# Second graph layer: gathered rows are weighted and split into high and low parts on VectorE and ScalarE, and one 512-column rounded matmul takes the place of the 256-column full-precision matmul with a weighted one-hot

## The chip, the cores and the metric

The kernel runs on one core of a Trainium2 chip. The metric is the device time of one execution in microseconds. Three runs of the kernel before gave 1801.48 (median), 1800.02 and 1804.83 us.

## The reference, cut to what matters

A graph of 3125 nodes with 256 features and 50,000 edges, sorted by destination, goes through two layers. The first is a typed attention layer with a residual and a layer norm. The second, which the change touches, is

```python
all_msg = jnp.einsum('nf,rfo->rno', h, weight)          # 16 relations
msg = all_msg[rel_type, src] * norm                     # norm: one weight per edge
gate = jax.nn.sigmoid(all_gate[rel_type, src])[:, None]
msg = msg * gate
agg = jax.ops.segment_sum(msg, dst, num_segments=n_nodes)
x = _layernorm(x + jax.nn.relu(agg))
```

## The kernel before, in words

Nodes are cut into 26 rounds of 121. An edge window of 2048 edges belongs to each round, 128 partitions by U = 16 "chunks" of one edge per partition. The kernel first builds tables, then runs the attention layer round by round, and on the way writes `message_table`: for each node and relation, the gated message of 256 f32 values. All of that stays as it was.

The second layer starts when the last messages are in the table. It is a loop of its own over the 26 rounds, written out in blocks of four turns (`Turn`, `turns`). The order on each engine is the order in which its block of code issues, and engines meet at semaphores alone. In each round:

- GpSimd (POOL, `gather_messages`, line 651) issues 16 indirect DMAs. Each takes its 128 row numbers from `rows` in on-chip memory and brings 128 rows of 1 KB from `message_table` into a chunk of `mrows`. `mrows` has LB = 4 buffers of a round each; before it fills one again, POOL waits until TensorE has done the round that used it (`l_agg`, `r.again`).
- VectorE (DVE, `weigh_onehot`, line 1524) builds, two rounds ahead, 16 weighted one-hot matrices of 128x121 with one TENSOR_SCALAR each: 1 where the edge's destination is this node, times the edge weight. It has four buffers too.
- TensorE (PE, `l1`, line 954) waits for each half of the round's rows, then sums the edges into nodes with 16 matmuls of f32 operands, 256 columns each. The trace shows two matmul records for each of these.
- `finish` (lines 1504 to 1515, DVE, with a square root on ScalarE, ACT, at line 1176) does relu, residual and layer norm of the round, and SyncE (SP) loads the residual and stores the result (`l1` and `last` in the SP block).

In the attention layer the same kinds of work stand beside each other: POOL gathers at line 637, DVE's `make_onehot` (line 1359) makes 16 one-hots in one operation from two broadcast operands, and `weigh` (line 1458) multiplies 128x1024 values four times in a row. `low_part` (line 1239) is the subtraction that makes the low part of a split, after ACT has copied the high part into a rounded type (`F32R`). The profile gives `mrows` the name of `kv`, the memory that it lies in.

## Time and profile before

| what | value |
|---|---|
| median of three runs | 1801.48 us |
| profiled execution, span | 1798.2 us |
| its own time beside the span | not given; the median run is 3.3 us longer than the span |
| second layer, first gather to end of span | 1179.3 to 1798.2 us |
| PE / DVE / ACT / POOL busy, whole span | 74% / 51% / 27% / 50% |
| gathers of the second layer | 416, of 0.951 us each, 1.25 us from start to start |
| matmul records of the second layer | 832, of 0.463 us each |

Busy shares are averages over stages with different limits; the second layer is read from stretches of its own. Waits named "remote" are for semaphores set by another engine whose work the profile doesn't pair with the wait. Some matmul records are missing from the trace, so that a PE which runs on without a break can look idle; PE's "issue" time in the second layer is mostly that.

### The profile page before, as it was taken

To read this page: it belongs to the slowest core of one execution; us is meant where nothing else is said; L and a number is where in the kernel's file an instruction comes from. 1 tells how busy PE (TensorE), PEld (TensorE's weight loads), DVE (VectorE), ACT (ScalarE), POOL (GpSimd) and SP (SyncE) were. 2 spreads that over 40 slices of the span, in tenths; PEclk is the share of its full clock that TensorE was granted. 3 is DMA by queue.
4 is the path that set the end of the run, shared out by engine and by line. 5 is a ranking of instruction groups with operands and counts; after the bars stand their busy time and mean duration, and the time that the engine had idled before them with its cause. 6 is when DMAs were issued, how large, how long until landed. Compare 5 with 4: busy or idle time off the path is not lost.

```text
span 1798.2 us, 21483 instructions
## 1 busy us (share of the span) xinstructions
PE 1322.6 (74%) x6758; PEld 1088.5 (61%) x6758; DVE 921.7 (51%) x1914; ACT 492.7 (27%) x1069; POOL 890.4 (50%) x905
## 2 busy tenths in 40 slices
PE   5799999458999999999999999943424444444444
PEld 4788888447878787878787888732313323332333
DVE  5744444468777777787878787221212222222222
ACT  3222222304454545454444444500000000000000
POOL 1041000476565656565656563057576666666661
PEclk9899999769999999999999999965556666666666
DMA  7454446566676767776767675333333333333331
GB/s 143 130 152 145 135 133 225 151 191 181 209 238 210 238 208 232 217 238 207 238 211 238 209 239 161 106 111 110 87 110 99 105 102 103 104 103 103 104 102 44
DMA packets 103851, 286.56 MB, mean 159 GB/s; under 512 B 20805, under 2 KB 40409, under 8 KB 100661
## 3 DMA queue, kind: packets, MB, share of 16 engines
q0 software_dynamic: 56032, 169.34, 31.5%
q1 hardware_dynamic: 47774, 116.71, 21.3%
q8 instruction: 19, 0.31, 0.1%
q14 instruction: 26, 0.20, 0.0%
HBM read 189.33 MB, written 96.65 MB: 159 GB/s over the span
## 4 chain that ended last, share of the span: by engine, by line
PE 56%; issue 24%; DVE 7%; DMA 6%; POOL 3%; ACT 1%; SPq 1%; another core or an unknown queue 1%; DVEq 0%; ACTq 0%; POOLq 0%
PE bank L954 14%; PE bank L837 11%; PE bank L865 10%; PE bank L795 5%; PE bank L729 5%; DMA kv_table<-tstage 4%; PE bank L783 2%; POOL kv L651 2%; PE bank L813 2%; PE bank L751 2%; PE bank L737 1%; DVE kv L1367 1%; PE bank L757 1%; POOL kv L637 1%; DVE S L1372 1%
## 5 line engine op out<-in xcount | busy, mean ns | idle before, releaser
L637 POOL DMA_INDIRECT kv<-kv_table,rows x416 | 458.6, 1102 | 304.9 <-PE bank L865 130.9
L651 POOL DMA_INDIRECT kv<-message_table,rows x416 | 395.7, 951 | 264.7 <-issue 123.5
L954 PE MATMUL bank<-kv,onehot_w 128*121 128x256 f32 x832 | 276.1, 463 | 336.7 <-issue 300.8
L954 PEld LDWEIGHTS bank<-kv,onehot_w 128*121 128x121 f32 x832 | 186.6, 226 | 426.2 <-issue 389.8
L837 PE MATMUL bank<-wr_r,x1T_r 128*121 128x512 f32 x1248 | 324.8, 403 | 2.2 <-ACT mstage L1098 2.2
L837 PEld LDWEIGHTS bank<-wr_r,x1T_r 128*121 128x121 f32 x1248 | 217.7, 183 | 51.9 <-ACT mstage L1098 3.3
L1504 DVE SCALAR_TENSOR_TENSOR z<-bank,xb 121x256 f32<-121x256 f32 x26 | 10.9, 420 | 429.7 <-remote 280.1
L1098 ACT ACTIVATE mstage<-bank,gate 121x256 f32<-121x256 f32 x416 | 171.0, 470 | 149.9 <-PE bank L837 137.3
L865 PE MATMUL bank<-kv,onehot_r 128*121 128x264 f32 x832 | 202.4, 392 | 0.0
L1176 ACT ACTIVATE sd<-mv,eps 121x1 f32<-121x1 f32 x26 | 7.7, 295 | 604.5 <-DVE mv L1510 513.4
L865 PEld LDWEIGHTS bank<-kv,onehot_r 128*121 128x121 f32 x832 | 150.3, 186 | 29.0
L1367 DVE TENSOR_TENSOR kv<-kv,bank 128x512 f32<-128x512 f32 x208 | 131.7, 674 | 47.4 <-PE bank L795 35.5
L795 PE MATMUL bank<-qb_r,onehotT_r 121*128 121x256 f32 x832 | 130.3, 301 | 14.6 <-DVE kv L1367 11.8
L1372 DVE TENSOR_REDUCE S<-kv 128x32 f32<-128x1024 f32 x104 | 127.1, 1222 | 10.7
L795 PEld LDWEIGHTS bank<-qb_r,onehotT_r 121*128 121x128 f32 x832 | 115.3, 199 | 19.8 <-issue 14.1
L1458 DVE TENSOR_TENSOR kv<-kv 128x1024 f32<-128x1024 f32 x104 | 120.4, 1220 | 12.8 <-ACT kv L1108 10.3
L1524 DVE TENSOR_SCALAR onehot_w<-iota_n,dstl,norms 128x121 f32<-128x121 f32 x416 | 111.1, 361 | 29.9 <-issue 18.5
L729 PE MATMUL bank<-xmT_r,w_r 128*128 128x484 f32 (+1 forms) x504 | 108.3, 377 | 10.5 <-DVE tstage L1299 8.4
L1056 ACT ACTIVATE onehotT_r<-bank 121x512 fp32r<-121x512 f32 x104 | 62.2, 598 | 178.0 <-PE bank L783 166.8
L729 PEld LDWEIGHTS bank<-xmT_r,w_r 128*128 128x128 f32 x504 | 91.8, 195 | 25.9 <-DVE tstage L1299 7.2
L751 PE MATMUL bank<-rel_r,kvT_r 128*121 128x384 f32 x312 | 65.1, 352 | 25.8 <-DVE kvT_r L1239 25.8
L783 PE MATMUL bank<-ident_r,onehot_r 128*121 128x128 f32 x416 | 71.3, 296 | 16.6 <-DVE onehot_r L1359 10.8
(135 smaller groups left out, 1397.7 us busy)
## 6 DMA issues: line engine op xcount, KB each, us to landing
message_table<-mstage SPq DMA_DIRECT2D x104, 484.0 KB
kv_table<-tstage SPq DMA_DIRECT2D x26, 1210.0 KB
kv<-kv_table,rows POOLq DMA_INDIRECT x416
kv<-message_table,rows POOLq DMA_INDIRECT x416
query_table<-qstage_r SPq DMA_DIRECT2D x26, 242.0 KB
qb_r<-query_table SPq DMA_DIRECT2D x26, 242.0 KB
kv<-in_Wr POOLq DMA_DIRECT2D x2, 2048.0 KB, 14.6
xb<-in_x SPq DMA_DIRECT2D x26, 121.0 KB
```

Source lines behind the costliest of these rows:

```text
L637: pool.indirect_dma_start(kv[:, n % 2, u, 0:2 * C], None, ktab, bass.IndirectOffsetOnAxis(ap=rows[:, 0, n, u:u + 1], axis=0)).then_inc(kv_ ...
L651: pool.indirect_dma_start(mrows[:, r.q, u, :], None, mtab, bass.IndirectOffsetOnAxis(ap=rows[:, 1, r.number, u:u + 1], axis=0)).then_inc(l ...
L729: last = mm(b[:, 0:plan.width], lhsT, rhs, start=(n == 0), stop=(n == len(terms) - 1))
L795: last = mm(b_qe[pr % 2][:, q * C:(q + 1) * C], onehotT_r[:, 2 * pr + q, :], qb_r[:, r.par, part, :], start=(part == 0), stop=(part == 1))
L837: last = mm(b_m[c % 2][:NODES, :], x1T_r[:, f.par, a, h, :], wr_r[:, w, h, 2 * c:2 * c + 2, :], start=(n == 0), stop=(n == len(terms) - 1))
L865: last = mm(b_agg[:NODES, 0:C + H], onehot_r[:, r.par, u, :].bitcast(F32), kv[:, r.par, u, C:ROW], start=(u == 0), stop=(u == U - 1))
L954: last = mm(b_l[r.q][:NODES, 0:C], onehot_w[:, r.q, u, :], mrows[:, r.q, u, :], start=(u == 0), stop=(u == U - 1))
L1098: last = a(mstage[:, b % 2, q % (RT // PARTS), :], b_m[c % 2][:NODES, k * C:(k + 1) * C], ACT.Copy, scale=gate[:NODES, f.par, q:q + 1])
L1367: ins = v.tensor_tensor(k, k, b_qe[pr % 2][:, :].rearrange("p (a c) -> p a c", a=2), ALU.mult)
L1372: v.tensor_reduce(S[:, :, u:u + 4].rearrange("p h u -> p u h"), kv[:, r.par, u:u + 4, 0:C].rearrange("p u (h d) -> p u h d", h=H), AX.X, A ...
L1458: v.tensor_tensor(w, w, e, ALU.mult).then_inc(weighted[g], 1)
L1524: last = v.tensor_scalar(onehot_w[:, r.q, u, :], iota_n[:, :], dstl[:, j, u], norms[:, j, u], ALU.is_equal, ALU.mult)
```

## The change

- DVE multiplies the gathered rows themselves by the edge weights, in place, one operation of 128x1024 for each quarter of a round (`weigh_rows`); ACT copies the product into the rounded type as its high part (`weigh_high`), and DVE subtracts that from the product to get the low part (`weigh_low`). High and low lie side by side in `rows_r`, which uses the memory of the message weights, and has two buffers.
- The one-hots are unweighted and rounded, made by one operation for each round (`mark`, one round ahead, two buffers).
- PE does one rounded matmul of 512 columns for each chunk: 256 high and 256 low sums. It waits quarter by quarter for `l_low`.
- ACT copies the low sums out of PSUM (`keep_low_sum`), DVE adds the high sums to them, and `finish` goes on from there. `finish` of a round now stands between the first quarter's `weigh_rows` and `weigh_low` of the next.
- Landings are counted by quarters, and POOL waits for `l_low` instead of `l_agg` before it fills a buffer again.

```diff
@@ Turn
-        return Turn(self.eng, self.i, self.q + 2) if self.q < 2 else Turn(self.eng, self.i + 1, self.q - 2)
+        return Turn(self.eng, self.i, self.q + 1) if self.q < LB - 1 else Turn(self.eng, self.i + 1, 0)
...
-            onehot_w = lsb("onehot_w", [P, LB, U, NODES])
+            onehot_w = lsb("onehot_w", [P, 1, U, NODES])
+            low_sum = hm[:, 0, :]
+            rows_r = wr_r[:, :, :, :, :].rearrange("p b h r c -> p b (h r) c").rearrange(
+                "p b (u k) c -> p b u k c", k=2)
@@ gather_messages (POOL)
-                    pool.wait_ge(l_agg, r.again)
+                    pool.wait_ge(l_low, G * r.again)
...
-                                            ).then_inc(l_landed[r.q][u * 2 // U], 16)
+                                            ).then_inc(l_landed[r.q][u // GU], 16)
@@ l1 (PE)
-                    if u % (U // 2) == 0:
-                        pe.wait_ge(l_landed[r.q][u * 2 // U], r.used)
-                    last = mm(b_l[r.q][:NODES, 0:C], onehot_w[:, r.q, u, :], mrows[:, r.q, u, :],
+                    if u % GU == 0:
+                        pe.wait_ge(l_low, r.parts(u // GU))
+                    last = mm(b_l[r.q][:NODES, 0:2 * C], onehot_r[:, r.par, u, :],
+                              rows_r[:, r.par, u, :, :].rearrange("p k c -> p (k c)"),
@@ ACT
+            def keep_low_sum(f):
+                act.wait_ge(l_agg, f.done)
+                wait(act, l_sum, f.halves(0))
+                a(low_sum[:, :], b_l[f.q][:NODES, C:2 * C], ACT.Copy).then_inc(l_sum, 1)
+
+            def weigh_high(r, g):
+
+                if g == 0 and r.reuses:
+                    act.wait_ge(l_agg, r.two_back)
+                act.wait_ge(l_weighed, r.parts(g))
+                u = slice(g * GU, g * GU + GU)
+                a(rows_r[:, r.par, u, 0, :], mrows[:, r.q, u, :], ACT.Copy).then_inc(l_high, 1)
+
+            def l1(r):
+                weigh_high(r, 0)
+                if not r.first:
+                    keep_low_sum(r.back())
+                    out_deviation(r.back())
+                for g in range(1, G):
+                    weigh_high(r, g)
@@ finish (DVE)
-                    sums = b_l[f.q]
                     dve.wait_ge(l_agg, f.done)
+                    b = b_l[f.q]
+                    dve.wait_ge(l_sum, f.halves(1))
+                    v.tensor_tensor(z[:NODES, :], b[:NODES, 0:C], low_sum[:, :], ALU.add).then_inc(l_sum, 1)
+                    dve.wait_ge(l_sum, f.halves(2))
+                    sums = z
@@ DVE
-            def weigh_onehot(r):
...
-                for u in range(U):
-                    last = v.tensor_scalar(onehot_w[:, r.q, u, :], iota_n[:, :], dstl[:, j, u], norms[:, j, u],
-                                           ALU.is_equal, ALU.mult)
-                last.then_inc(l_oh, 1)
+            def mark(r):
+
+                if r.reuses:
+                    dve.wait_ge(l_agg, r.two_back)
+                d = dstl[:, bass.ds(r.number, 1), :].rearrange("p j u -> p (j u)").unsqueeze(2).broadcast_to([P, U, NODES])
+                v.tensor_tensor(onehot_r[:, r.par, :, :], iota_n[:, :].unsqueeze(1).broadcast_to([P, U, NODES]), d,
+                                ALU.is_equal).then_inc(l_oh, 1)
+
+            def weigh_low(r, g):
+
+                dve.wait_ge(l_high, r.parts(g))
+                u = slice(g * GU, g * GU + GU)
+                v.tensor_tensor(rows_r[:, r.par, u, 1, :], mrows[:, r.q, u, :], rows_r[:, r.par, u, 0, :].bitcast(F32),
+                                ALU.subtract).then_inc(l_low, 1)
+
+            def weigh_rows(r, g):
+
+                dve.wait_ge(l_landed[r.q][g], r.used)
+                u = slice(g * GU, g * GU + GU)
+                w = norms[:, bass.ds(r.number, 1), u].rearrange("p j u -> p (j u)").unsqueeze(2).broadcast_to([P, GU, C])
+                v.tensor_tensor(mrows[:, r.q, u, :], mrows[:, r.q, u, :], w, ALU.mult).then_inc(l_weighed, 1)
 
             def l1(r):
-                if not (isinstance(r.i, int) and r.number + 2 >= ROUNDS):
-                    weigh_onehot(r.ahead())
-                finish(r)
+                weigh_rows(r, 0)
+                if not r.first:
+                    finish(r.back())
+                weigh_low(r, 0)
+                if not (isinstance(r.i, int) and r.number + 1 >= ROUNDS):
+                    mark(r.ahead())
+                for g in range(1, G):
+                    weigh_rows(r, g)
+                    weigh_low(r, g)
```

A check of how full the windows are (`fill`, three tiny operations before the attention layer) changes only which semaphore it steps on.

## Rows read from the trace of the kernel before

**Rows 1.** Stretches: length, busy us (count) by engine, PE's granted clock, DMA.
```profile
1179.00:1770.00 591.00, 261.41 (x765) 174.44 (x766) 135.83 (x490) 6.78 (x23) 395.66 (x416) 0.63 0.35 102
```
**Rows 2.** Waits of the second layer: us in total, times, longest.
```profile
POOL kv L651 <- remote: 64.0, 10, 12.3
```
**Rows 3.** The same view of stretches, one swing of PE's clock in the second layer.
```profile
1309.00:1364.00 55.00, 17.43 (x36) 9.92 (x36) 9.90 (x37) 0.59 (x2) 36.00 (x39) 0.50 0.33 96
1364.00:1377.00 13.00, 10.66 (x49) 8.62 (x47) 7.42 (x28) 0.29 (x1) 9.93 (x11) 1.00 0.49 138
```
**Rows 4.** One line's instructions: duration ns min/median/max, first and last start.
```profile
L651 POOL DMA_INDIRECT kv<-message_table,rows x416: 943/949/1052, 1179.3 to 1761.5; - x139
```
**Rows 5.** Timeline of POOL and PE early in the second layer: start, duration, work.
```profile
1188.12 0.95 POOL L651 DMA_INDIRECT kv<-message_table,rows  x1 [0.30 <-issue]
...
1190.98 6.29 PE L954 MATMUL bank<-kv,onehot_w 128*121 128x256 f32 x16 [19.12 <-DMA kv<-message_table,rows]
```
**Rows 6.** Timeline at the end of the attention layer and in it: PE's message matmuls.
```profile
1165.86 6.01 PE L837 MATMUL bank<-wr_r,x1T_r 128*121 128x512 f32 x24 [0.42 <-ACT mstage L1098]
```
**Rows 7.** Groups by shape: line, operation, shapes, count, busy us, mean ns, idle before.
```profile
L1458 DVE TENSOR_TENSOR kv<-kv 128x1024 f32<-128x1024 f32 x104 | 120.4, 1220 | 12.8 <-ACT kv L1108 10.3 <-issue 2.5
L1359 DVE TENSOR_TENSOR onehot_r<-iota_n,dstl 128x1936 fp32r<-128x1936 f32 x26 | 56.5, 2172 | 0.0
L1397 DVE TENSOR_TENSOR z<-z,bank 121x256 f32<-121x256 f32 x26 | 11.0, 422 | 46.6 <-PE bank L813 27.2 <-issue 19.4
L1239 DVE TENSOR_TENSOR w_r<-w_in,w_r 128x1536 fp32r<-128x1536 f32 x3 | 5.2, 1757 | 0.8 <-ACT w_r L1003 0.7
```
**Rows 8.** The same view for ACT's copies into the rounded type.
```profile
L1038 ACT ACTIVATE qstage_r<-bank 121x256 fp32r<-121x256 f32 x26 | 10.0, 384 | 46.9 <-PE bank L737 43.9 <-DMA query_table<-qstage_r 3.1
L1003 ACT ACTIVATE w_r<-w_in 128x1536 fp32r<-128x1536 f32 x3 | 4.3, 1479 | 6.4 <-DMA w_in<-in_Wk 6.4
L1013 ACT ACTIVATE ident_r<-ident 128x128 fp32r<-128x128 f32 x1 | 0.3, 298 | 0.0
```
**Rows 9.** Timeline of DVE, ACT and POOL in one round of the attention layer.
```profile
1035.08 2.17 DVE L1359 TENSOR_TENSOR onehot_r<-iota_n,dstl 128x1936 fp32r<-128x1936 f32 x1
...
1035.85 2.22 POOL L637 DMA_INDIRECT kv<-kv_table,rows  x1 [0.31 <-issue]
...
1039.63 0.95 POOL L637 DMA_INDIRECT kv<-kv_table,rows  x1 [0.30 <-issue]
1039.67 0.29 DVE L1450 TENSOR_TENSOR S<-S,masks 128x128 f32<-128x128 f32 x1
1040.45 4.63 DVE L1458 TENSOR_TENSOR kv<-kv 128x1024 f32<-128x1024 f32 x4 [0.49 <-issue]
...
1040.88 1.61 POOL L637 DMA_INDIRECT kv<-kv_table,rows  x1 [0.30 <-issue]
...
1042.80 1.97 POOL L637 DMA_INDIRECT kv<-kv_table,rows  x1 [0.31 <-issue]
```
**Rows 10.** Timeline of the last round's finish.
```profile
1784.75 0.42 DVE L1504 SCALAR_TENSOR_TENSOR z<-bank,xb 121x256 f32<-121x256 f32 x1 [4.77 <-PE bank L954]
1785.20 0.43 DVE L1507 BATCH_NORM_STATS2 st<-z 121x6 f32<-121x256 f32 x1
1785.73 0.18 DVE L1510 BATCH_NORM_AGGREGATE mv<-st 121x2 f32<-121x6 f32 x1
1785.95 0.29 ACT L1176 ACTIVATE sd<-mv,eps 121x1 f32<-121x1 f32 x1 [6.62 <-DVE mv L1510]
1786.28 0.16 DVE L1512 RECIPROCAL rstd<-sd 121x1 f32<-121x1 f32 x1 [0.36 <-ACT sd L1176]
1786.48 0.41 DVE L1515 TENSOR_SCALAR x<-z,mv,rstd 121x256 f32<-121x256 f32 x1
```
**Rows 11.** Timeline of one gather that is slow by 0.10 us, and its DVE neighbour.
```profile
1099.23 0.29 DVE L1450 TENSOR_TENSOR S<-S,masks 128x128 f32<-128x128 f32 x1
1099.29 1.05 POOL L637 DMA_INDIRECT kv<-kv_table,rows  x1 [0.30 <-issue]
```

More of the change, by code:

```diff
@@ L121, in stores_before, with halves, parts, first @@
         return self.i * (16 * LB) + 16 * (self.q - 2)
+    def halves(self, k):
+        return self.i * (2 * LB) + (2 * (self.q - 2) + k)
+    def parts(self, g):
+        return self.i * (LB * G) + ((self.q - 2) * G + g + 1)
+    @property
+    def first(self):
+        return isinstance(self.i, int) and self.number == 0
+    @property
+    def reuses(self):
+        return not (isinstance(self.i, int) and self.number < 2)
     def ahead(self):
-        return Turn(self.eng, self.i, self.q + 2) if self.q < 2 else Turn(self.eng, self.i + 1, self.q - 2)
+        return Turn(self.eng, self.i, self.q + 1) if self.q < LB - 1 else Turn(self.eng, self.i + 1, 0)
+    def back(self):
+        return Turn(self.eng, self.i, self.q - 1) if self.q else Turn(self.eng, self.i - 1, LB - 1)
 def turns(eng, body):
@@ L316, in build @@
         oh_ready = sem("oh_ready")
-        kv_landed = [sems(f"kv_landed{p}_", G) for p in range(2)]
+        rows_landed = [sems(f"rows_landed{q}_", G) for q in range(LB)]
+        kv_landed, l_landed = rows_landed[0:2], rows_landed
         ohT_filled, ohT_ready = sems("ohT_filled", G), sems("ohT_ready", G)
@@ L336, in build @@
         x1_stored = sem("x1_stored")
-        l_oh, l_agg = sem("l_oh"), sem("l_agg")
-        l_landed = [sems(f"l_landed{q}_", 2) for q in range(LB)]
+        l_oh, l_weighed, l_high, l_low, l_agg = (sem(n) for n in ("l_oh", "l_weighed", "l_high", "l_low", "l_agg"))
         l_x = sems("l_x", 2)
@@ L1313, in _ @@
             v.tensor_scalar(fill[:, ROUNDS - 1:], starts[:, ROUNDS - 1:], -1.0, float(E), ALU.mult, ALU.add)
-            v.tensor_tensor(fill[:, 0:ROUNDS - 1], starts[:, 1:], starts[:, 0:ROUNDS - 1], ALU.subtract).then_inc(fill_ready, 1)
-            dve.wait_ge(fill_ready, 1)
-            v.tensor_reduce(most[:, :], fill[:, :], AX.X, ALU.max).then_inc(fill_ready, 1)
-            dve.wait_ge(fill_ready, 2)
+            link(v.tensor_tensor(fill[:, 0:ROUNDS - 1], starts[:, 1:], starts[:, 0:ROUNDS - 1], ALU.subtract))
+            link(v.tensor_reduce(most[:, :], fill[:, :], AX.X, ALU.max))
             v.tensor_scalar(overfull[:, :], most[:, :], -float(ROUND_EDGES), 0.0, ALU.add, ALU.max).then_inc(overfull_ready, 1)
@@ L1537, in _ @@
+            mark(Turn(dve, 0, 2))
             turns(dve, l1)
+            finish(Turn(dve, QUADS, LB - 1))
             with general(dve):
```

21 lines of the change are left out of this document (10 added, 11 removed).

## The prediction

> **What bounds the kernel now.** I read the stretches first, then the waits, then the timeline. The second layer runs from its first gather at 1179.3 us to the end of the span at 1798.2, a third of the time, and the change is in this part alone. In it POOL is the busiest engine by the records: 395.66 of 591 us [rows 1]. One gather holds POOL for 0.95 us and is followed by 0.30 us of idle time [rows 4, 5], so gathers go out every 1.25 us, or more closely 20.06 us for the 16 of a round. 416 of them would take 521.6 us. The last one starts at 1761.5 [rows 4], and 1761.5 + 0.9 - 1179.3 = 583.1 us. The difference, 61.5 us, is POOL's 64.0 us of waits for PE to free a buffer [rows 2] (64.0 counts the 0.30 before each of them too). Per round: 583.1 / 26 = 22.4 us.
>
> Why PE is late is seen in its clock: over 55 us it is granted 0.50 (1.2 GHz), then over 13 us 1.00 (2.4 GHz), again and again [rows 3]. At the low clock PE takes longer for 16 pairs of matmuls than POOL for 16 gathers, falls four rounds behind and works without a break until the clock rises, then catches up, waits for rows, and the clock falls. So the bound is POOL's 20.06 us with about 2.4 us a round of PE's low clock on top.
>
> **The change part by part.**
>
> PE. 32 matmul passes of 256 columns a round become 16 of 512. In the attention layer 24 rounded matmuls of 512 columns took 6.01 us in a row [rows 6], 0.25 us each. Sixteen are 4.0 us a round; at half that clock 8.0. This is far under 20 us, so the 61.5 us of waits go, whatever the clock is. What is late next is the question.
>
> DVE. The 16 small one-hot operations go. In their place stand, for each quarter, a product of 128x1024 values and a subtraction of 128x1024, and for each round one `mark` of 128x1936. The nearest rows are 1.22 us for the product and 2.17 us for the mark, which are the same operations on the same shapes; the subtraction is L1239's, 1.757 us at 1536 values, and at the slope between these rows (2.172 - 1.757 over 400 values, 1.04 ns each) 1.22 us at 1024 [rows 7]. The sum of high and low halves is one 121x256 addition with a PSUM operand, 0.42 us [rows 7]. Eight times 1.22 + 2.17 = 11.9 us; with finish's five operations (0.42 + 0.43 + 0.18 + 0.16 + 0.41) and the addition, 13.9 us a round.
>
> ACT. A copy of 1024 values into the rounded type: 0.298 us at 128 and 1.479 at 1536 [rows 8] give 0.839 ns a value and 1.05 us at 1024. The low sum's copy is 0.38 us [rows 8]. From one engine to the next 0.03 to 0.04 us pass (1785.91 to 1785.95 and 1786.24 to 1786.28) [rows 10].
>
> The chain in a quarter is product, copy, subtraction: 1.22 + 0.03 + 1.05 + 0.03 + 1.22 = 3.56 us. In the first quarter finish stands between the two: it starts when ACT is through with the copy and the low sum (1.5 us after the product), takes 0.42 + 0.42 + 0.43 + 0.18 + 0.29 + 0.16 + 0.41 and some 0.3 of steps, so the quarter's subtraction starts 4.1 us after the product and the mark ends 3.3 us after that. A round of DVE: 1.22 + 4.1 + 3.3 + 3 x 3.56 = 19.3 us. That is just under POOL's 20.06, so DVE's own queue doesn't set the pace as long as a round takes longer than this.
>
> POOL. The number of gathers and their size stay; the wait for `l_low` of four rounds back never holds, since DVE is at most some 4 us behind a landing. But gathers don't keep their 0.95 us beside every DVE operation. In the attention layer one takes 2.22 us: it starts at 1035.85, inside the one-hot operation that runs from 1035.08 to 1037.25, and ends at 1038.07, 0.82 us after that. Beside the four products in a row (starts 1.14 apart) one starts at 1040.88, in the first, which ends at 1041.67, and itself ends at 1042.49, again 0.82 later. The next starts at 1042.80, just after the third product began (1042.72), and ends at 1044.77, 0.83 after that product's end at 1043.94. A gather that starts 0.04 us before a DVE operation with two inputs in on-chip memory (1039.63 against 1039.67) is not slowed [rows 9]; one that starts 0.06 us after such an operation's start is [rows 11]. So: a gather whose start falls inside such an operation waits for its end, and then takes 0.82; the loss is (end of the operation - start of the gather - 0.13). In the second layer of before there are no long ones of this kind, and the slowest gather is 1.05 us [rows 4]. The change puts 11.9 us of them into each round, all in the time of the gathers: product (rows and weights), subtraction (product and high part), mark (as L1359). This is the step that decides.
>
> The Trainium skill ("SBUF — State Buffer", section "Who interferes with whom") says that a DVE instruction with two SBUF inputs contends with a GpSimd instruction that reads SBUF. It also says there that `tensor_tensor` was not seen to stall a DMA's descriptor generation, since that needs the write side. By the first sentence the stalls come, by the second there are none and the gathers stay at 20.06 us a round. The 2.22 us gather speaks for the first, as these gathers read their row numbers.
>
> **The price of the stalls.** From both sides: nothing, if none of the gathers starts in such an operation; and at most 8 x (1.22 - 0.13) + (2.17 - 0.13) = 10.8 us a round. At random phases a 1.22 us operation costs 1.09 x 1.09 / (2 x 1.25) = 0.47 us and the mark 2.04 - 0.63 = 1.41 us, together 5.2. The phases are not random, since DVE starts when rows land. I walk a round from the end of the last gather of a quarter (0). The following gathers start at 0.30, 1.56 and 2.81. The quarter's rows have landed 1.9 us after 0 (gather 8 ends at 1189.07, PE starts on it at 1190.98 [rows 5]).
> - The product runs from 1.9 to 3.1 and meets the gather of 2.81, which loses 0.1 to 0.2 us.
> - That one ends 0.82 after the product, and the next gather starts 0.30 later, 1.12 us after the product's end. The subtraction starts 0.03 + 1.05 + 0.03 = 1.12 us after the product's end. This is a tie within 0.01 us. If the subtraction is first, the gather loses 1.22 - 0.13 - 0.01 = 1.08; if the gather is first, nothing, and the subtraction is over (2.34) before the next gather (2.37).
> - In the quarter with finish and mark, the subtraction meets a gather somewhere in its middle (0.4), and the next starts 1.12 us after the subtraction's end, 1.1 us before the mark's end, and loses 0.9: 1.3 together.
> - After the mark DVE is behind and goes on without waiting for rows. The same spacing comes back: each gather let go by one operation is followed by one that starts about when the next operation does. Of the three plain quarters' subtractions I therefore take each as a toss of its own, worth 1.06 us.
>
> So a round takes 20.06 + 2 x 0.13 + 1.3 + n x 1.06 = 21.6 + 1.06 n, with n from 0 to 3: 21.6, 22.7, 23.7, 24.8. Before it was 22.4. I take n = 3: the rows put a start that is 0.06 after the operation's start on the losing side, and 0.04 before it on the winning side; the reckoned tie has the subtraction first by 0.01, and the random-phase sum (25.3) lies nearest to it.
>
> **Sum.** First gather 1179.3. Gathers: 26 x 24.8 = 644.8. Then the last quarter: landing 1.9, chain 3.56, four matmuls at the low clock 2.0, low sum 0.45, finish 2.6, together 10.5. From the end of the last normalization (1786.89) to the span's end are 11.3 us [rows 10], which stay. Span 1179.3 + 644.8 + 10.5 + 11.3 = 1845.9; the median run is 3.3 us over the span before, so **1849 us**, 2.6% slower. The tail alone gains: before, from the end of the last gather (1762.4) to 1786.9 are 24.5 us of PE's backlog, now 10.5. Equal time would be at 23.0 us a round.
>
> **The rivals.**
> - Gather first (n = 0 or 1): ACT's copy takes a little longer than reckoned, so the next gather has started before the subtraction does. It decides at a copy of about 1.06 us against the 1.05 reckoned. A round is 21.6 or 22.7 us, the time 1766 or 1794: faster than before, by up to 2%. For it: the copy writes in four blocks, and no row shows what that adds. Against: rows 8 show nothing near it. It is the rival of the other sign.
> - Part of the subtractions lose (n = 2): 1821 us.
> - No stall at all, since POOL's write side is what counts: 1179.3 + 521.3 + 10.5 + 11.3 + 3.3 = 1726 us. The Trainium skill's second sentence above would give this. Against it stand all the slow gathers of rows 9.
> - DVE becomes the bound: its operations wait for POOL as well, or the chain takes longer than 3.56. With stalls at random phases, 25.3 us a round, the time is 1862; with 0.2 us more for each quarter's chain it doesn't change, since 19.3 + 0.8 is still under the round. Only above 24.8 us of DVE time a round would it pass my sum.
> - PE still late at the low clock: 8.0 us a round against 20 speaks against it; 5 us would have to be lost for each quarter.
>
> **How the numbers follow.** n = 3 has a chance of 0.45 (1849), n = 2 0.17 (1821), n = 0 or 1 0.22 (1766 to 1794), no stall 0.06 (1726), worse than my sum 0.10 (1862 and above). The likeliest one's own range is 1838 to 1862. For 8 in 10 the range goes from 1766, the best tossed case, to 1868, a little above random phases; it leaves out the case of no stall and the tail of the last one. This kernel can be told from no change from about 0.3% on, 5.4 us. Slower is all of n = 2, 3 and worse, less what chance there is of n near 1.3 (1801): 0.69. Faster is the rest but a narrow band: 0.27; within 0.3%: 0.04.
>
> **What would show it right or wrong.** In the profile after: POOL's gathers at the same line with a mean of about 0.95 + (24.8 - 20.06) / 16 = 1.25 us instead of 0.951, and single ones near 2.0; no wait of POOL for a buffer; products and subtractions of 1.22 us, the mark at 2.17, ACT's copy at 1.05; PE at 1.2 GHz for nearly all of the layer and mostly idle. It is wrong in the step of the tie if the mean of a gather is under 1.12 (n of 1 or less), in the step of the stall if it is 0.95, and in the step of DVE's queue if DVE stands busy or waiting on ACT all the time while POOL waits for `l_low`.

## The result: 0.65% slower, and the profile after

| what | before | after |
|---|---|---|
| median (runs, span of times) | 1803.15 us (4, 1800.02 to 1805.81) | 1813.75 us (4, 1812.88 to 1815.52) |
| ratio after / before | | 1.0065, 95% interval 1.0052 to 1.0077 |
| profiled execution, span | 1798.2 us | 1811.9 us (its own time 1814.03) |

The forecast was 1849 us, inside a range of 1766 to 1868: the sign was right, the size was not. The stretch of the second layer, in the view of [rows 1] (length, busy us (count) of PE, weight load, DVE, ACT and POOL, granted clock, DMA share, GB/s):

```profile
1182.00:1791.00 609.00, 211.54 (x411) 115.63 (x412) 349.48 (x381) 124.24 (x154) 481.85 (x416) 0.50 0.34 99
```

POOL's busy time rose from 396 to 482 us, PE's fell from 261 to 212 and DVE's rose from 136 to 349. PE has the low clock, 0.50 (1.2 GHz), throughout. POOL's waits, against [rows 2]:

```profile
POOL kv L677 <- issue: 126.5, 415, 0.3
```

The 64.0 us of waits for a buffer are gone; all that is left is 0.30 us ahead of each gather. The line itself, against [rows 4], and DVE's and ACT's new work, against [rows 7, 8] (mean ns in the second number after the bar):

```profile
L677 POOL DMA_INDIRECT kv<-message_table,rows x416: 942/947/2912, 1182.1 to 1789.5; - x139
```
```profile
L677 POOL DMA_INDIRECT kv<-message_table,rows x416 | 481.9, 1158 | 202.1 <-issue 126.5 <-DMA message_table<-mstage 75.7
L980 PE MATMUL bank<-wr_r,onehot_r 128*121 128x512 f32 x411 | 211.8, 667 | 404.7 <-DVE wr_r L1582 338.1 <-issue 66.6
L1582 DVE TENSOR_TENSOR wr_r<-kv,wr_r 128x1024 fp32r<-128x1024 f32 x103 | 126.9, 1232 | 87.5 <-ACT wr_r L1216 87.5
L1590 DVE TENSOR_TENSOR kv<-kv,norms 128x1024 f32<-128x1024 f32 x103 | 125.8, 1221 | 122.5 <-DMA kv<-message_table,rows 122.5
L1216 ACT ACTIVATE wr_r<-kv 128x1024 fp32r<-128x1024 f32 x103 | 108.8, 1056 | 444.9 <-DVE kv L1590 332.0 <-PE bank L980 95.7 <-issue 17.2
L1575 DVE TENSOR_TENSOR onehot_r<-iota_n,dstl 128x1936 fp32r<-128x1936 f32 x25 | 54.2, 2167 | 0.0
```

The median gather is as before, the mean is 1.158 us: a few gathers of each round are long. Which ones is seen in the timeline of DVE and POOL over one round, from its first quarter's subtraction:

```profile
1498.92 1.22 DVE L1582 TENSOR_TENSOR wr_r<-kv,wr_r 128x1024 fp32r<-128x1024 f32 x1
...
1500.06 2.17 DVE L1575 TENSOR_TENSOR onehot_r<-iota_n,dstl 128x1936 fp32r<-128x1936 f32 x1
...
1501.27 1.78 POOL L677 DMA_INDIRECT kv<-message_table,rows  x1 [0.30 <-issue]
1502.14 1.21 DVE L1590 TENSOR_TENSOR kv<-kv,norms 128x1024 f32<-128x1024 f32 x1
1503.35 0.95 POOL L677 DMA_INDIRECT kv<-message_table,rows  x1 [0.30 <-issue]
...
1504.48 1.22 DVE L1582 TENSOR_TENSOR wr_r<-kv,wr_r 128x1024 fp32r<-128x1024 f32 x1 [1.12 <-ACT wr_r L1216]
1504.60 1.92 POOL L677 DMA_INDIRECT kv<-message_table,rows  x1 [0.30 <-issue]
1505.62 1.22 DVE L1590 TENSOR_TENSOR kv<-kv,norms 128x1024 f32<-128x1024 f32 x1
...
1507.96 1.22 DVE L1582 TENSOR_TENSOR wr_r<-kv,wr_r 128x1024 fp32r<-128x1024 f32 x1 [1.12 <-ACT wr_r L1216]
1508.08 1.92 POOL L677 DMA_INDIRECT kv<-message_table,rows  x1 [0.30 <-issue]
...
1511.92 1.23 DVE L1590 TENSOR_TENSOR kv<-kv,norms 128x1024 f32<-128x1024 f32 x1 [2.73 <-DMA kv<-message_table,rows]
1512.81 1.15 POOL L677 DMA_INDIRECT kv<-message_table,rows  x1 [0.30 <-issue]
...
1514.26 1.26 DVE L1582 TENSOR_TENSOR wr_r<-kv,wr_r 128x1024 fp32r<-128x1024 f32 x1 [1.12 <-ACT wr_r L1216]
1514.27 0.95 POOL L677 DMA_INDIRECT kv<-message_table,rows  x1 [0.30 <-issue]
```

Two subtractions, at 1504.48 and 1507.96, start 0.12 us ahead of a gather and hold it: 1.92 us, a loss of 0.97 each. The third, at 1514.26, starts 0.01 ahead, and the gather takes its usual 0.95. The other losses of a round are 0.20 and 0.22 us beside products (1512.81 is one), 0.33 and 0.83 beside the first quarter's subtraction and the mark. Together 3.5 us. The last gather ends at 1790.5, so the 26 rounds take (1790.5 - 1182.1) / 26 = 23.4 us each; every "us a round" of a whole run below is worked out in this way. The end, against [rows 10]:

```profile
1792.46 1.22 DVE L1590 TENSOR_TENSOR kv<-kv,norms 128x1024 f32<-128x1024 f32 x1 [2.91 <-DMA kv<-message_table,rows]
...
1800.89 0.41 DVE L1567 TENSOR_SCALAR x<-z,mv,rstd 121x256 f32<-121x256 f32 x1
```

The account of the 13.7 us between the spans: first gather 2.9 later (1182.1 against 1179.3), gathers 25.2 longer (608.3 against 583.1), last gather to last normalization 13.7 shorter (10.8 against 24.5), the rest 0.7 shorter (10.6 against 11.3). The 2.9 are not the change's: the part ahead of the first gather is the same, and in the runs below that gather starts anywhere from 1177.9 (e2) to 1183.7 (e20).

### The profile page after: what moved, and what is told of

It reads as the page before. It is cut to its first block, busy times and chain, and to the rows that moved or that the text cites. A ratio compares the mean times of both kernels' runs of the same rounds, so it can differ in the third digit from the quotient of the medians.

```text
span 1811.9 us, 20676 instructions
## 1 busy us (share of the span) xinstructions
PE 1261.8 (70%) x6342; PEld 1019.7 (56%) x6342; DVE 1126.2 (62%) x1758; ACT 610.5 (34%) x1199; POOL 975.4 (54%) x905
## 4 chain that ended last, share of the span: by engine, by line
PE 40%; POOL 28%; issue 14%; DVE 8%; DMA 6%; ACT 1%; SPq 1%; another core or an unknown queue 1%; DVEq 0%; ACTq 0%; POOLq 0%
POOL kv L677 27%; PE bank L863 11%; PE bank L891 10%; PE bank L755 5%; PE bank L821 5%; DMA kv_table<-tstage 4%; PE bank L809 2%; PE bank L777 2%; DVE kv L1415 2%; PE bank L763 1%; DVE S L1420 1%; POOL kv L663 1%; PE bank L839 1%; PE bank L783 1%; DMA x_all<-in_x 1%
## 5 line engine op out<-in xcount | busy, mean ns | idle before, releaser
L677 POOL DMA_INDIRECT kv<-message_table,rows x416 | 481.9, 1158 | 202.1 <-issue 126.5
L980 PE MATMUL bank<-wr_r,onehot_r 128*121 128x512 f32 x416 | 214.3, 667 | 409.2 <-DVE wr_r L1582 342.5
L980 PEld LDWEIGHTS bank<-wr_r,onehot_r 128*121 128x121 f32 x416 | 116.8, 311 | 506.4 <-DVE wr_r L1582 378.1
L1216 ACT ACTIVATE wr_r<-kv 128x1024 fp32r<-128x1024 f32 x104 | 109.8, 1056 | 450.3 <-DVE kv L1590 337.5
L1590 DVE TENSOR_TENSOR kv<-kv,norms 128x1024 f32<-128x1024 f32 x104 | 127.0, 1221 | 125.4 <-DMA kv<-message_table,rows 125.4
L1582 DVE TENSOR_TENSOR wr_r<-kv,wr_r 128x1024 fp32r<-128x1024 f32 x104 | 128.1, 1232 | 88.6 <-ACT wr_r L1216 88.6
```

The source lines that it names most:

```text
L677: pool.indirect_dma_start(mrows[:, r.q, u, :], None, mtab, bass.IndirectOffsetOnAxis(ap=rows[:, 1, r.number, u:u + 1], axis=0)).then_inc(l ...
L980: last = mm(b_l[r.q][:NODES, 0:2 * C], onehot_r[:, r.par, u, :], rows_r[:, r.par, u, :, :].rearrange("p k c -> p (k c)"), start=(u == 0), ...
L1582: v.tensor_tensor(rows_r[:, r.par, u, 1, :], mrows[:, r.q, u, :], rows_r[:, r.par, u, 0, :].bitcast(F32), ALU.subtract).then_inc(l_low, 1)
L1590: v.tensor_tensor(mrows[:, r.q, u, :], mrows[:, r.q, u, :], w, ALU.mult).then_inc(l_weighed, 1)
```

## The experiments

The kernel before stood at 1798 to 1803 us beside them; ratios are to it, with the 95% interval behind them. Theory 1 is the prediction's: apart from gathers that DVE holds, the 16 gathers of a round take their own 20.0 us and nothing else is late.

### Does PE's low clock make the kernel before late? (e1)

```diff
-                    last = mm(b_l[r.q][:NODES, 0:C], onehot_w[:, r.q, u, :], mrows[:, r.q, u, :],
+                    if u % 2:
+                        last = mm(b_l[r.q][:NODES, 0:C], onehot_w[:, r.q, u, :], mrows[:, r.q, u, :],
```

> The kernel before, with the matmuls of every second chunk of the second layer left out, so that half of the edges are not summed. It tests the first step: that PE at its low clock, and nothing else, adds to POOL's gathers before the change. If so, PE needs 11 us or less a round against POOL's 20.06, POOL never waits for a buffer, and the layer is 416 x 1.254 = 521 us of gathers and a short tail: about 1726 us. If POOL's waits for l_agg had another cause (landings, the finish), the time stays near 1803.

Measured: 1789.93 us (ratio 0.9931, 0.9912 to 0.995). Not 1726: half of PE's work is gone, and POOL still waits for PE nearly as long as before (view of waits; 64.0 in [rows 2]):

```profile
POOL kv L651 <- remote: 57.0, 6, 12.6
```

So PE's speed is not what makes it late. In this kernel's timeline one sees the other engines slow too, DVE for instance:

```profile
1527.17 0.95 POOL L651 DMA_INDIRECT kv<-message_table,rows  x1 [0.30 <-issue]
...
1528.07 0.34 DVE L1525 TENSOR_SCALAR onehot_w<-iota_n,dstl,norms 128x121 f32<-128x121 f32 x1 [0.39 <-issue]
...
1529.46 0.34 DVE L1525 TENSOR_SCALAR onehot_w<-iota_n,dstl,norms 128x121 f32<-128x121 f32 x1 [1.05 <-issue]
```

Two operations of 0.34 us that wait for nothing start 1.39 us apart, while POOL's gathers keep their pace. I call such a stretch, in which all engines but POOL crawl or stand, a late stretch.

### Moving the tie (e2, e3, e19, e20)

```diff
 e2: the subtraction starts 0.09 us later (1.21 us after the product's end in place of 1.12)
-                a(rows_r[:, r.par, u, 0, :], mrows[:, r.q, u, :], ACT.Copy).then_inc(l_high, 1)
+                a(rows_r[:, r.par, u, 0, :], mrows[:, r.q, u, :], ACT.Copy)
+                a(unused[:, :], eps[:, :], ACT.Copy).then_inc(l_high, 1)
 e3: ACT copies 248 of 256 columns (8 columns of the high part are left out)
-                a(rows_r[:, r.par, u, 0, :], mrows[:, r.q, u, :], ACT.Copy).then_inc(l_high, 1)
+                a(rows_r[:, r.par, u, 0, 0:248], mrows[:, r.q, u, 0:248], ACT.Copy).then_inc(l_high, 1)
```

> The kernel after, with one tiny ACT operation (about 0.2 us) behind each quarter's copy, and the signal to DVE given by it, so that each subtraction starts about 0.15 to 0.2 us later. Theory 1 (a gather that starts inside a DVE operation with two SBUF inputs waits for its end): in the kernel after, two of the four subtractions of a round start 0.12 us before the next gather and cost it 0.97 us each; started later they come behind it and cost nothing. A round gets shorter, from 23.4 to about 21.5 us, and the time falls to about 1765 us, though each of the 104 chains is longer. Theory 2 (the length of the chain on DVE and ACT sets the round): 104 x 0.15 to 0.2 us more, about 1830 to 1835. Theory 3 (gathers are slowed by something that has nothing to do with when DVE operations start): no change, 1814.

Measured: 1786.96 us (0.9935, 0.991 to 0.996). One more operation in every quarter's chain makes the changed kernel 27 us faster: 22.5 us a round, mean gather 1.10 us. The timeline of e2:

```profile
1510.64 1.28 DVE L1583 TENSOR_TENSOR wr_r<-kv,wr_r 128x1024 fp32r<-128x1024 f32 x1 [1.21 <-ACT unused L1217]
1510.67 0.94 POOL L677 DMA_INDIRECT kv<-message_table,rows  x1 [0.30 <-issue]
1511.85 1.21 DVE L1591 TENSOR_TENSOR kv<-kv,norms 128x1024 f32<-128x1024 f32 x1
1511.91 1.96 POOL L677 DMA_INDIRECT kv<-message_table,rows  x1 [0.30 <-issue]
```

The subtraction no longer holds a gather. Theory 1's time is missed by some 20 us because now a product, 0.06 us ahead of a gather, holds one for 1.0 us.

> The kernel after, with ACT's copy of the high part 248 columns wide instead of 256 in each chunk, so that it is about 0.027 us shorter; the last 8 columns of the high part are not written. Theory 1: in the one quarter of a round in which subtraction and gather start together (both at 1204.02, at 1514.26), the subtraction now starts first, and the gather loses about 1.08 us: 26 x 1.08 = 28 us more, about 1842 us. Theory 2 (the chain's length): 104 x 0.027 = 3 us less, 1811. Theory 3: no change, 1814.

Measured: 1810.06 us (1.0052, 1.0033 to 1.007): a miss. The subtraction now leads the gather by 0.03 us in place of 0.01, and the gather is still free:

```profile
1507.85 0.95 POOL L677 DMA_INDIRECT kv<-message_table,rows  x1 [0.30 <-issue]
```

The 1810 are near theory 2's 1811, but e2, where each chain got longer and the time shorter, speaks against theory 2.

> The kernel of e2 with ScalarE's copy in two halves of 128 columns of each chunk, so that l_high comes some 0.2 us later again (two starts in place of one). In e2 one product of each round still starts 0.06 us before a gather and holds it for 1.0 us. Theory 1 (only held gathers count): the product moves to after the gather, rounds of 21.5 us, 1760. Theory G (with fewer held gathers the late stretches come back, as in e15 and e16, where rounds of 21.5 and 20.4 us alternate with long ones): 1785 to 1815, however few gathers are held.

```diff
 e20: e2, and the copy in two halves
+                a(rows_r[:, r.par, u, 0, 0:C // 2], mrows[:, r.q, u, 0:C // 2], ACT.Copy)
+                a(rows_r[:, r.par, u, 0, C // 2:C], mrows[:, r.q, u, C // 2:C], ACT.Copy)
```

Measured: 1793.49 us (0.9942, 0.9926 to 0.9959), 22.6 us a round, POOL waits for no buffer. Theory 1 had the product come free, and it did not:

```profile
1518.08 0.94 POOL L677 DMA_INDIRECT kv<-message_table,rows  x1 [0.30 <-issue]
1518.14 1.23 DVE L1584 TENSOR_TENSOR wr_r<-kv,wr_r 128x1024 fp32r<-128x1024 f32 x1 [1.31 <-ACT unused L1218]
1519.29 1.22 DVE L1592 TENSOR_TENSOR kv<-kv,norms 128x1024 f32<-128x1024 f32 x1
1519.33 2.00 POOL L677 DMA_INDIRECT kv<-message_table,rows  x1 [0.30 <-issue]
```

Two DVE operations in a row start 1.15 us apart, two free gathers 1.25. So where DVE is behind, a subtraction that comes 0.06 after a gather brings the next product 0.04 ahead of the next gather, and that holds it. The time lies in theory G's range, but for another reason: late stretches did not come back, since gathers are still held. It tells nothing of G.

> The kernel of e2 once more, as the version that was faster than both kernels: 1787 us, 0.993 of the kernel before, 0.985 of the changed one (1813.8).

Measured: 1789.76 us, ratio 0.992 (0.9906 to 0.9934). With e2 this is the fastest kernel here that does all the work: 0.7% to 0.8% faster than before, 1.3% faster than the change by the medians. Its rounds are no shorter than those of the kernel before (22.5 against 22.4 us): what it gains is the end, 21.4 us behind the last gather in e2 against 35.8 before.

### No held gathers (e6, e8, e9), and shorter operations (e7)

```diff
 e6: norms, iota and the product lie in PSUM: no DVE operation of a quarter has two inputs in on-chip SBUF memory
-                w = norms[:, bass.ds(r.number, 1), u]...
-                v.tensor_tensor(mrows[:, r.q, u, :], mrows[:, r.q, u, :], w, ALU.mult).then_inc(l_weighed, 1)
+                wait(dve, l_low, r.parts(g - 1))
+                w = p_norms[:, bass.ds(r.number, 1), u]...
+                v.tensor_tensor(product, mrows[:, r.q, u, :], w, ALU.mult).then_inc(l_weighed, 1)
```

> The kernel after, with the numbers 0 to 120, all edge weights and the quarter's product held in PSUM, so that product, subtraction and mark each have one input from SBUF and one from PSUM; the work is the same. Theory 1: none of them stalls a gather any more, each gather takes 0.95 us, a round 20.06 us, and the time is about 1182 + 521 + 11 + 11 + 2 = 1727 us, below both kernels. A variant of it: DVE's own round of 19.3 us or more, with the added steps, passes 20.06, POOL waits for l_low, and the time is 1730 to 1750. Theory 3 (it isn't the inputs' place): no change, 1814.

Measured: 1887.39 us (1.0488, 1.0458 to 1.0518), 160 us over theory 1. The first half of it is confirmed and the second refuted. The line and POOL's waits in e6:

```profile
L682 POOL DMA_INDIRECT kv<-message_table,rows x416: 940/946/1036, 1181.0 to 1804.2; - x139
```
```profile
POOL kv L682 <- issue: 126.1, 409, 1.8
POOL kv L682 <- DVE wr_r L1587: 104.6, 6, 24.2
```

No gather is held: this shows the stall mechanism, since DVE's operations are the same in number, size and duration (1.22 to 1.23 us each), and only where the product, the weights and the node numbers lie has changed, with one wait of the product for the subtraction before it. But POOL waits 104.6 us in six times for DVE, and 75 us of work lie behind the last gather. The timeline around one of these:

```profile
1500.67 2.06 PE L985 MATMUL bank<-wr_r,onehot_r 128*121 128x512 f32 x4 [1.69 <-issue]
...
1518.34 0.38 ACT L1213 ACTIVATE hm<-bank 121x256 f32<-121x256 f32 x1 [15.24 <-remote]
1518.75 0.43 DVE L1557 TENSOR_TENSOR z<-bank,hm 121x256 f32<-121x256 f32 x1 [16.71 <-remote]
```

and the same 16 us in the view of stretches:

```profile
1502.00:1518.00 16.00, 0.74 (x2) 0.01 (x1) 0.04 (x1) 1.02 (x1) 12.04 (x14) 0.50 0.36 106
```

PE's matmuls are over at 1502.7 by the records, and the signal that the round is done reaches ACT and DVE 15.6 us later. Only POOL works. This is a late stretch again, and since DVE's own chain takes 19.7 us a round (e12 below) against 20.0 of POOL, almost nothing of it is caught up.

> The run with everything in PSUM, and POOL waits before the third and fourth quarter of a round until the first and second have landed (they have, 5 us before, so the wait costs nothing by itself). Theory 4a (POOL's unbroken row of gathers holds up PE's signals, and any wait instruction in the row breaks it): the late signals go, a round takes 20.06 us, and the time is about 1727 us. Theory 4b (only time in which POOL really rests helps): 1887 as before. Theory 5 (the late signals have to do with the PSUM layout, not with POOL): 1887.

> The run with everything in PSUM, with one tiny memset on POOL before each quarter of gathers (0.09 us of work, some 0.15 to 0.2 us with its gap): four a round. Theory 4a: late signals go, a round takes 20.7 us, the time is about 1743 us. Theory 4b: little or no change from 1887, since a pause of 0.2 us is no rest. Theory 5: 1887 plus 16.

```diff
 e8: POOL, ahead of the third and fourth quarter
+                    if u % GU == 0 and u >= 2 * GU:
+                        pool.wait_ge(l_landed[r.q][u // GU - 2], r.used)
 e9: POOL, ahead of each quarter; e10 the same in the kernel before
+                    if u % 4 == 0:
+                        pool.memset(spare[...one column...], 0.0)
```

Measured: 1886.82 us (1.046) and 1886.3 us (1.0463): no change from e6. One memset of 0.12 us disappears in the 0.30 us ahead of a gather, so the pace is that of e6. Theory 4a has fallen. Theory 5 (the PSUM layout) is not told apart by e8; it falls with e7, which has late stretches without that layout, and with e12 and e15, which keep the layout and lose most of them.

> The kernel after, without the products of 128x1024: ACT copies each chunk with the edge weight as its scale (high part), and DVE makes the low part of each chunk by one operation of 128x256 (row times weight minus high part); only the mark stays long. Theory 1 (a gather that starts inside a DVE operation with two SBUF inputs waits for its end): the operations are 0.42 us instead of 1.22, so a gather can lose 0.3 us at most where it lost up to 1.08; some 0.15 us for each quarter, and 1.1 for the mark. A round takes 20.06 + 0.6 + 1.1 = 21.8 us, the time is about 1770 us. Theory 4, new from the run with everything in PSUM (there the gathers were not stalled, but the signal of PE's last matmul of a round came up to 26 us late, and the time rose): while POOL issues its gathers without a break, the other engines are held up. Under it a round nearly free of stalls can be slower than one with them: over 1800 us, with POOL waiting for a buffer.

e7 has no product: ACT copies each chunk with the weight as its scale, and DVE's low part of a chunk is one `scalar_tensor_tensor` of 128x256. Measured: 1849.98 us (1.0258, 1.0233 to 1.0283). Theory 1 missed by 80 us, theory 4 (over 1800) came true. The gathers were not free here: line 677 took 941/947/4450 ns, 1.096 us in the mean, some 62 us more than in e6 over all. Theory 1's loss of 0.3 us at most was wrong, because the short operations follow each other without a gap, and a gather that starts among them waits for the end of the whole row (one that started at 1554.34 took 4.45 us, beside twelve operations from 1553.13 to 1557.96). Rounds of 20.0 us stand beside four of 27 to 36 us, and ACT and DVE wait for PE's signal as in e6 (view of waits, 1370 to 1520: ACT 117.2 us in four times).

### What the late stretches come from (e10 to e18)

> The kernel before, with the same four tiny memsets a round on POOL. By the theory of my prediction (PE at its low clock is too slow) nothing changes but POOL's time: about 1803 us. By theory 4a PE's stalls go: at the low clock 32 matmul records of 0.43 us are 13.7 us a round, less than POOL's 20.7, POOL doesn't wait for buffers, and the time is about 1745 us.

Measured: 1799.38 us (0.998, 0.996 to 0.9999), no change to speak of. That is near the 1803 of the prediction's theory and far from the 1745 of theory 4a; of the gathers' pace it says nothing, since e9's four memsets did not change it.

> The kernel of e6 (no VectorE operation of a quarter with two inputs from SBUF), with the second layer's loop over quarters, and SyncE's loop over rounds, written out: every wait has a constant, no engine jumps or computes a register. In e6 the gathers were never held by a VectorE operation (946 ns each, 20.0 us a round), yet TensorE came 7 to 26 us late once every few rounds. Theory L (the late stretches come of the loops: an engine that must fetch its instructions again after a jump, or whose register operations take 0.7 us there): they go, 22 rounds of 20.0 us for the second layer, 1727 us (the same sum as for e6), at any rate under 1780. Theory G (they come of the gathers, whose descriptors are written without a pause and take something that the other engines' instructions need): no change, 1880 to 1895. Theory N (neither; writing out makes the program longer and the instructions have to be fetched as before): also about 1887, or slower.

> The kernel before, with the loops of the second layer written out in the same way. Theory L: the 5.5 us that GpSimd loses once in two rounds go (some 2.4 us a round, 22 rounds), about 1750. Theory G: 1803, no change.

> The changed kernel with the loops of the second layer written out. Its rounds are set by GpSimd's held gathers (23.4 us), by both theories: 1810 to 1818, unless the phase between VectorE and GpSimd moves by a few hundredths of a us, in which case one or two of the three held gathers of a round are free and it is 1770 to 1795.

```diff
 e11, e13, e14: in turns(); the SyncE loop in the same way
-    with eng.Fori(2, QUADS) as i:
-        for q in range(LB):
-            body(Turn(eng, i, q))
+    for n in range(2, ROUNDS + 2):
+        body(Turn(eng, n // LB, n % LB))
```

Measured: e11 1877.52 us (1.0438, 1.0397 to 1.0478), e13 1806.25 (1.0039, 1.0017 to 1.0061), e14 1807.9 (1.0061, 1.0039 to 1.0082). Theory L has fallen: the late stretches stay in e11 (98.3 us of POOL's waits in 7 times) and in e13 (68.0 us in 13). e11 and e14 came out 2 to 3 us under what was expected of them without L. Theory N (the engines wait for instructions to be brought in) is not touched by e11, but the trace of e6 speaks against it: from 1480 to 1530 us, around the late stretch shown, the view of DMA queues lists the gathers' queue and SyncE's, and neither of the two instruction queues, which have 17 packets between them from 1181 to 1880 us. (The "22 rounds" in the expectations of e11 and e13 is a slip for 26; by 26 L's time for e13 is about 1740.)

> The kernel of e6 with only the first two of the four gathers of each quarter issued: half of the edges use the rows that stand in the buffers from before, and the landing counts are halved; all work of the other engines stays. Theory G (the late stretches come of GpSimd writing descriptors without a pause): they go, the second layer is then bound by VectorE or by the others at their own pace; from e6's VectorE rows that is some 19 us a round, and 1690 to 1720 in all. Theory L (loops, instruction fetch): the late stretches stay where they are, as the others run the same program, and the time is 1850 or more.

```diff
 e12: half of the gathers left out
+                    if u % GU >= 2:
+                        continue
```

Measured: 1718.95 us (0.9571, 0.9542 to 0.9599). The late stretches are gone but for one of 10.8 us, which falls among the first rounds, before POOL has waited for a buffer, while it still issues every 1.25 us. POOL now waits for DVE (197.0 us), and DVE sets 39.4 us for two rounds:

```profile
DVE z L1559 <- remote: 10.8, 1, 10.8
```

The other engines run the same program as in e6, which took 168 us more. So the gathers make the late stretches: theory G. Its two forms:

> The kernel of e6 with all gathers issued, each for rows of 128 columns in place of 256 (half of the bytes of the gathers; the other half of each buffer keeps old values). Theory Ga (the late stretches come of GpSimd writing descriptors without a pause): same descriptors, same time as e6, 1887. Theory Gb (they come of the rows' landing, that is of the traffic of the DMA engines into SBUF): they go as in e12, and the gathers' own pace of 20.0 us a round gives 1182 + 26 x 20.0 + 11 = 1713 to 1730.

```diff
 e18: rows of 128 columns, the same number of gathers and rows
-                    pool.indirect_dma_start(mrows[:, r.q, u, :], None, mtab,
+                    pool.indirect_dma_start(mrows[:, r.q, u, 0:C // 2], None, mtab.rearrange("r (h c) -> (r h) c", h=2),
```

Measured: 1892.32 us (1.0511, 1.0479 to 1.0543), waits as in e6:

```profile
POOL kv L682 <- DVE wr_r L1587: 116.6, 7, 24.4
```

So it is the number of gathers or of their rows, not the bytes; the gathers' queue takes 17.9% of the DMA engines' time from 1480 to 1530 us against 30.4% in e6. Gb in this form has fallen. Ga (what POOL does for a gather) fits, but work of the DMA engines that goes by the row is not ruled out. And their pace:

> The kernel of e6 with four small GpSimd memsets (32 partitions, one column each) ahead of each quarter's gathers. In e9 one such memset (0.12 us) fitted into the 0.30 us that lie between two gathers anyway and did not slow the gathers; four of them take some 0.5 us and so add 0.2 to 0.5 us a quarter: rounds of 20.9 to 22.0 us. Theory G (the late stretches appear when GpSimd issues gathers 1.25 us apart without an interruption, as e12 with half of the gathers had none): they go, and the 26 rounds give 1182 + 26 x 21.4 + 11 = 1750 us (1736 to 1765). If the pace has to be slower than this for them to go: still 1850 or more.

> The same with two memsets a quarter, that is 0 to 0.15 us more a quarter and rounds of 20.1 to 20.7 us. Theory G with a threshold at the bare pace: 1725 to 1745. With a threshold at some pace between 20.0 and 22.6 us a round (e2 ran at 22.6 without late stretches): 1840 to 1887.

> The kernel before with the same four memsets a quarter. Theory G for the kernel before too (its 2.4 us a round that GpSimd waits for TensorE are late stretches of the same kind and not a matter of TensorE's clock): they go, rounds of 20.9 to 22.0 us, 1736 to 1765 us. Theory of the prediction (TensorE is too slow at its low clock and the round's length is its own): the round stays at 22.4 us, and the memsets hide in GpSimd's waits: 1803.

```diff
 e15, e17: ahead of each quarter's gathers; e16 with range(2)
+                    if u % GU == 0:
+                        for k in range(4):
+                            pool.memset(spare[32 * k:32 * k + 32, ...one column...], 0.0)
```

Measured: e15 1793.67 us (0.9957, 0.9941 to 0.9972), e16 1855.29 (1.0281, 1.0235 to 1.0326), e17 1803.8 (1.001, 0.9989 to 1.0031). Sixteen tiny memsets a round on the engine that issues the gathers make e6 faster by 94 us, eight by 32; e16 lies in the range that its text gives for a threshold at some pace. So the pace matters, and steeply: 20.0 us a round undisturbed gives 1887, 20.4 gives 1855, 21.5 gives 1794. But e15 did not give the 1736 to 1765 that I expected. At 21.5 us a round there are still longer rounds of 24 us between, and there POOL itself stands, waiting for nothing (e15):

```profile
1501.85 0.22 POOL L685 MEMSET spare<- 32x1 f32 x2
...
1503.98 0.09 POOL L685 MEMSET spare<- 32x1 f32 x1 [1.92 <-issue]
1504.69 0.09 POOL L685 MEMSET spare<- 32x1 f32 x1 [0.61 <-issue]
```

e17 decides nothing. Its 1803.8 us are the 1803 of the prediction's theory, and theory G's 1736 to 1765 did not come. POOL's 64.0 us of waits for PE [rows 2] shrink to 12.7 and 19.5, but the memsets cost what was won (22.8 us a round in place of 22.4), and both theories have the memsets take the place of waits:

```profile
POOL spare L654 <- issue: 19.5, 30, 1.4
POOL spare L654 <- remote: 12.7, 4, 3.7
```

That the 2.4 us a round of the kernel before come of late stretches is better seen in its own trace, in the timeline around one of POOL's waits (1490.1 to 1495.6):

```profile
1466.64 0.34 DVE L1524 TENSOR_SCALAR onehot_w<-iota_n,dstl,norms 128x121 f32<-128x121 f32 x1 [1.00 <-issue]
1468.03 0.34 DVE L1524 TENSOR_SCALAR onehot_w<-iota_n,dstl,norms 128x121 f32<-128x121 f32 x1 [1.05 <-issue]
...
1488.29 0.58 PE L954 MATMUL bank<-kv,onehot_w 128*121 128x256 f32 x1 [2.22 <-issue]
1491.09 0.58 PE L954 MATMUL bank<-kv,onehot_w 128*121 128x256 f32 x1 [2.22 <-issue]
```

DVE's operations of 0.34 us start 1.39 us apart, as in e1, and PE's matmuls of 0.58 us start 2.80 apart; neither waits for anything. I had put such idle time of PE down to missing records, but the 832 records are all there: 26 rounds of 32.

One regularity of the late stretches stands in the trace of e6, before POOL has waited for the first time. It is ACT's first copy after each of them (timeline of ACT):

```profile
1235.34 0.38 ACT L1213 ACTIVATE hm<-bank 121x256 f32<-121x256 f32 x1 [5.51 <-remote]
1280.14 0.38 ACT L1213 ACTIVATE hm<-bank 121x256 f32<-121x256 f32 x1 [25.27 <-remote]
1324.94 0.38 ACT L1213 ACTIVATE hm<-bank 121x256 f32<-121x256 f32 x1 [25.27 <-remote]
```

They end 44.80 us apart, and 36 gathers start between one and the next. e18, with rows of half the size, has the same distances (1236.71, 1281.54, 1326.34), again of 36 gathers. What repeats there, no run tells.

## Why the prediction was right in sign and wrong in size

- **What bounds before.** That POOL's gathers bound the kernel, with 2.4 us a round on top, was right. That the 2.4 come of PE's low clock was wrong, and my own rows said so: at the low clock 36 records took 17.43 us of 55 [rows 3], so a round's 32 take 15.5 us, under POOL's 20, and PE did not work "without a break". I took the low clock that I saw beside the late stretch for its cause; e1, with half the matmuls and 57.0 us of waits, shows that it is not. In the rows the clock is low where PE is busy for 17.43 of 55 us and high where it is busy for 10.66 of 13.
- **What the change removes.** The waits are gone, as forecast, and the tail lost 13.7 us against 14.0 reckoned. But for the waits that was luck: they were to go because PE needs 8.0 us a round at most, and e6, whose PE does the same work, has 104.6 us of them. They go in the changed kernel while its gathers are held, and come back when they are not.
- **Durations.** Product 1.221 us (1.22), subtraction 1.232 (1.22), mark 2.167 (2.17), copy 1.056 (1.05). Four 512-column matmuls in a row took 2.06 us (2.0).
- **The stall.** Right, and now shown by e6: gathers of 946 ns in the mean, 1036 at most, once DVE has no two inputs in SBUF. The loss formula gives 1.22 - 0.12 - 0.13 = 0.97, measured 0.97. Of the Trainium skill ("SBUF — State Buffer", section "Who interferes with whom"), the sentence on two SBUF inputs holds here, and what it says of `tensor_tensor`, that it was not seen to stall a DMA's descriptor generation, does not hold for these indirect gathers (1.92 against 0.95 us).
- **The tie.** This is the step that failed: "Of the three plain quarters' subtractions I therefore take each as a toss of its own", and all three taken as lost. Only two a round were (n = 2, for which the text had 23.7 us a round and 1821; it is 23.4 and 1813.75). By the text's own mark for a wrong tie (a mean gather under 1.12 us) the step would have passed, with 1.158. They are no tosses, the same two are lost each time. In the two quarters after the mark DVE is behind, one gather starts at the product's end (1503.35) and the next 1.25 later, and the subtraction, 1.13 later, is 0.12 ahead: lost each time. Only in the last quarter is the tie as reckoned (a lead of up to 0.01 us; the prediction's sum of 0.03 + 1.05 + 0.03 is 1.11, not 1.12, and 1.12 was measured), and there such a lead is not enough to hold the gather. The rows had only "0.06 after" on the losing side; e3 shows that 0.03 is still free, e20 that 0.04 is not (by starts shown to 0.01). The third loss, 1.06 us a round or 27.6 us, is most of the miss of 35.3. The other terms of a round were each a little off: 0.97 for each of the two losses and not 1.06, 1.16 for the first quarter and not 1.3, 20.0 for the bare gathers and not 20.06, 0.42 for the products and not 0.26. With these the rounds take 36.5 us less than forecast; the later first gather (2.9) and smaller terms outside the rounds make it 35.3.
- **The rivals.** "Gather first" was described as faster than before by up to 2%. e2 is near its condition (the plain quarters' subtractions are free) and is 0.7% faster, not 2%, since a product is held in their place. The rival "no stall at all", 1726 us, was not reached by any run: the kernel without held gathers runs into late stretches (1887). The held gathers of the changed kernel cost 3.5 us a round. That they also keep the late stretches away by slowing the gathers is argued from e6, e15 and e16, where the pace alone was changed; it was not shown by itself.

What stays open is what the gathers take from the other engines. The loops are ruled out (e11), the bytes too (e18), DVE's hold on the gathers also (e6 has none). Whether it is POOL's own work on a gather or the DMA engines' work on its rows was not told apart, nor why a signal of PE is 15 us late.

## What to carry to other kernels

When one engine issues gathers back to back, write down the start of each gather and of each VectorE operation with two SBUF inputs on one time axis before adding up durations: here a VectorE start 0.04 us ahead of a gather's cost 1 us, one 0.03 us ahead nothing, and an operation more in the chain made the kernel faster. Don't put an engine's lateness down to a low clock beside it; halve its work first. When a forecast effect comes true, ask whether its cause did too: the waits went, and not for the reason given. And don't count on the issuing engine's full rate: here no version whose gathers ran undisturbed came near the sum of their durations.

## What the runs showed of the hardware that I had not expected

- With gathers of 128 rows issued every 1.25 us without a break, all other engines stand or crawl for up to 25 us now and then (e6: six waits of POOL, 104.6 us; before and e1: operations of 0.34 us 1.39 us apart). With a round 7.5% longer (21.5 against 20.0 us) they lose far less (1794 against 1887 us), with half of the gathers almost nothing (1719).
- A gather and a DVE operation that start within 0.03 us of each other run side by side, and the DVE operation then takes 0.04 to 0.06 us longer (1.26 and 1.28 against 1.22). From 0.04 us of lead on it holds the gather (e20).
- A gather that starts among short DVE operations with inputs in SBUF, one behind the other without a gap, is held to the end of the whole row: 4.45 us in e7, with operations of 0.48 us.
